# Dealing the two free PSUM banks of an attention by a fixed rule instead of in turns

## The reference, cut to what matters

```python
x = L0_attn_in_features                                # (8, 512, 256)
xn = _layernorm(x)
x = x + _L0_attn_ref(xn, ...) + _L0_ffn_ref(xn, ...)   # causal softmax attention; experts
xn = _layernorm(x)
x = x + _L1_attn_ref(xn, ...) + _L1_ffn_ref(xn, ...)   # gated recurrence; experts

def _L0_attn_ref(in_features, Wq, Wk, Wv, Wo):         # 16 heads of 16
    q, k, v = split_heads(xn @ Wq.T), ...
    scores = einsum('bhsd,bhtd->bhst', q, k) / 4       # causal mask
    out = einsum('bhst,bhtd->bhsd', softmax(scores), v)
    return out @ Wo.T
```

## Time and profile before

| | |
|---|---|
| time, median of 3 runs | 1647.87 us (1644.03 to 1649.47) |
| the profiled execution | 1642.28 us, span 1640.5 us |
| mean granted TensorE clock | 0.979 |
| TensorE busy | 1536.9 us (94%) |
| VectorE busy | 861.1 us (52%) |
| ScalarE busy | 733.3 us (45%) |
| GpSimd busy | 713.8 us (44%) |

### The profile page before, as it was taken

How to read it: one execution, slowest core, us unless ns; L and a number is a source line. 1 busy time by engine, 2 the same in 40 slices (tenths; PEclk the granted TensorE clock), 3 DMA queues, 4 the chain that set the end, 5 groups by cost and what they waited for, 6 DMA issues and landing times.

```text
span 1640.5 us, 32489 instructions
## 1 busy us (share of the span) xinstructions
PE 1536.9 (94%) x10874; PEld 1180.9 (72%) x10874; DVE 861.1 (52%) x2424; ACT 733.3 (45%) x1923; POOL 713.8 (44%) x815
## 2 busy tenths in 40 slices
PE   5888989999999999999988799998999999999997
PEld 3445445555547999998655467767999899999996
DVE  5777897787822444442577778874322122222220
ACT  4544545555551232333556466644333333334332
POOL 3132336676532555553810467753333333333332
PEclk9899999999999999999998999999999999999999
DMA  8534324435306444444622386467333333333331
GB/s 271 126 115 110 79 73 98 104 94 102 83 4 240 108 113 114 113 114 130 204 92 67 103 219 105 79 105 290 59 56 52 51 56 54 55 58 59 53 55 23
DMA packets 154640, 167.60 MB, mean 102 GB/s; under 512 B 84821, under 2 KB 132817, under 8 KB 151409
## 3 DMA queue, kind: packets, MB, share of 16 engines
q1 hardware_dynamic: 129936, 128.15, 31.5%
q0 software_dynamic: 24544, 37.38, 10.6%
HBM read 104.10 MB, written 44.45 MB: 91 GB/s over the span
## 4 chain that ended last, share of the span: by engine, by line
PE 78%; DVE 10%; DMA 4%; issue 3%; ACT 3%; SPq 1%; POOL 0%; another core or an unknown queue 0%; DVEq 0%; ACTq 0%; POOLq 0%
PE PS L1660 23%; PE PS L1678 22%; PE PS L1517 4%; PE PS L1453 3%; PE PS L1767 3%; DVE PS L1980 3%; PE PS L1502 3%; PE PS L1481 2%; PE PS L1634 2%; PE PS L1543 2%; PE PS L1588 2%; PE PS L1779 2%; PE PS L1463 1%; PE PS L1865 1%; DMA arena<-FD 1%
## 5 line engine op out<-in xcount | busy, mean ns | idle before, releaser
L1660 PEld LDWEIGHTS PS<-arena 128*128 128x128 f32 x3408 | 398.2, 192 | 16.3 <-DVE arena L2201 4.9
L1660 PE MATMUL PS<-arena 128*128 128x128 f32 x3408 | 405.3, 276 | 3.5 <-DVE arena L2201 3.5
L1678 PE MATMUL PS<-arena 128*128 x1704 | 392.3, 379 | 0.0
L1678 PEld LDWEIGHTS PS<-arena 128*128 128x128 f32 x1704 | 311.9, 190 | 40.1 <-issue 0.2
L1980 DVE CUSTOM_DVE_ANT_0 PS<-PS,arena 128x512 f32<-128x512 f32 (+3 forms) x512 | 235.2, 522 | 50.7 <-PE PS L1481 47.2
L995 POOL DMA_INDIRECT out<-arena x71 | 111.7, 1573 | 296.4 <-ACT arena L1272 274.0
L1262 ACT ACTIVATE arena<-PS,arena 128x128 f32<-128x128 f32 x568 | 161.8, 368 | 138.3 <-PE PS L1660 136.5
L2226 DVE COPY arena<-arena 128x8 f32 x71 | 12.2, 172 | 347.5 <-ACT arena L1262 326.3
L928 POOL TENSOR_SCALAR_AFFINE_SELECT arena<-arena 128x256 f32<-128x256 f32 x256 | 99.4, 411 | 204.0 <-ACT arena L1178 203.7
L981 POOL DMA_INDIRECT arena<-XN,arena x142 | 145.0, 1021 | 98.6 <-PE PS L1645 40.6
L1178 ACT ACTIVATE arena<-PS 128x512 f32<-128x512 f32 (+1 forms) x256 | 166.5, 705 | 42.1 <-PE PS L1502 34.4
(11 more groups left out here) (246 smaller groups left out, 2014.3 us busy)
## 6 DMA issues: line engine op xcount, KB each, us to landing
arena<-FD SPq DMA_DIRECT2D x32, 512.0 KB
arena<-in_w SPq DMA_DIRECT2D x16, 1024.0 KB
SPL<-arena SPq DMA_DIRECT2D x32, 384.0 KB, 2.6
arena<-SPL SPq DMA_DIRECT2D x64, 192.0 KB
XN<-arena SPq DMA_DIRECT2D x16, 512.0 KB, 3.0
arena<-SPL SPq DMA_DIRECT2D x64, 128.0 KB
arena<-SUM SPq DMA_DIRECT2D x16, 512.0 KB, 6.4
arena<-in_x SPq DMA_DIRECT2D x8, 512.0 KB, 6.6
```

Source lines behind the costliest of these rows:

```text
L1660: ins = pe.matmul(o, m.now[i % 2][:, c * F + 128 * f:c * F + 128 * f + 128], m.xt[i % 2][:, 128 * c:128 * c + 128], start=(c == 0), stop=( ...
L1678: ins = pe.matmul(to, m.hT[i % len(m.hT)][:, 128 * c:128 * c + 128], m.WD[:, bass.ds(e * (nf * 256) + c * 256, 256)], start=(c == 0), stop ...
```

## The change

A table gives each kind of small step a fixed bank; a kind with two entries takes the one of its last index (half or m). It holds from the step after the last `logitsT` on. Up to there, and for kinds that are not in the table, the turns are as before.

```diff
+OWN = {"scale": (7,), "project": (6, 7), "unscaleT": (7,), "maxrow": (6,), "output": (6, 7), "project_v": (6, 7)}
@@ def attention_banks(order):
-    uses, ring = Uses(), [4, 5, 6, 7]
+    uses, ring, own = Uses(), [4, 5, 6, 7], {}
     for step in order:
         if step[0] == "two_banks":
             ring = [7, 6]
             uses.at[step] = tuple(uses.count[b] for b in (4, 5))
+        elif step[0] in own:
+            uses.take(step, own[step[0]][step[-1] if len(own[step[0]]) > 1 else 0])
         elif step[0] in ("xt0", "xt1", "logits", "logitsT", "project", "project_v", "maxrow", "scale", "unscaleT", "output", "first_up", "first_down"):
             ring.append(ring.pop(0))
             uses.take(step, ring[-1])
+            if step == ("logitsT", NB - 1):
+                own = OWN
         elif step[0] == "values":
             uses.take(step, 6)
```

## The result

The changed kernel takes 1634.22 us (median of 11 runs, 1630.32 to 1638.53). The kernel before, run beside it, takes 1644.03 us (11 runs, 1636.31 to 1649.47). The ratio is 0.995, with a 95% interval from 0.9931 to 0.9968: 8.2 us gained, between 5.3 and 11.3. The forecast was 1642.2 us with a range from 1637 to 1648. Faster was right; the time lies under the range. The profiled execution took 1631.14 us (span 1629.4, clock 0.979), which is 11.1 us less than the one of before.

The account below looks back on a forecast made before the run. TensorE was taken to bound most of the first attention, VectorE weighing as much before it. Gains of 0.35 + 0.38 + 5.0 = 5.7 us off the 1647.87 us median gave 1642.2 us, range 1637 to 1648.

Parts of the forecast that it names:

- cost zero: Second project, bank 6 to 7: its new wait for the unscaleT copy delays nothing, with some 0.24 us of cover.
- values: Values in each round of 8 heads: the 0.36 us bank wait goes, and 0.33 us passes on through VectorE's gap.
- output, project_v: First output or project_v half of each round, bank 7 to 6: its 0.38 us wait goes in full.
- So the two gains add: Per round of 8 heads, the values' 0.33 us and the output's 0.38 us sum to 0.71 us.
- 7 rounds of 0.71 = 5.0 us: Gain claimed for the even stretch of the first attention, from 250 to 420 us.
- VectorE takes over: Rival, chance 0.13: VectorE swallows the values' gain everywhere, leaving 3.4 us gained, 1644.5 us.
- The early part: Before 250 us: the project at 174.46 gains 0.35 us, project_v at 185.8 gains 0.38, the rest taken as 0.
- Values at 180 us ... buys nothing: Before 250 us: VectorE has no gap from 178.78 to 188, so these values' 0.37 us gains nothing.
- Clock gains: Rival, chance 0.17: half-speed loss avoided at 174 us (1.7 us) or also later; 7.4 or 9.8 us gained, 1638 to 1640.5.
- Clock loses: Rival, chance 0.10: longer idling at the routing's end slows one more stretch by 2.4 us; 3.3 us gained, 1644.6.
- The new wait binds: Rival, chance 0.05: second project waits 1.07 us for the unscaleT copy at ten places; net 5.0 us slower, 1652.9.
- It does nothing: Rival, chance 0.05: the named releasers are wrong and data hold the same steps; 1647.9 us.

Follow-up runs that it names:

- e2: Kernel before with only the values' bank wait undone (both projects on bank 7); ratio to before 0.9993, slots 48–108 in 177.76 us.
- e1: Kernel before with only the second project's own bank wait undone; ratio to before 0.9984, slots 48–108 in 179.02 us.
- e3: Kernel before with only the output and project_v bank wait undone (halves on 6 and 7); ratio to before 0.9971, slots 48–108 in 176.87 us.
- e5: Kernel before with the values' and the output or project_v waits undone, the project's kept; 1639.37 us, slots 48–108 in 174.21 us.
- e4: Changed rule only from head slot 49 on, behind the routing, banks of before until then; ratio to before 0.9962, slots 48–108 in 173.79 us.
- e6: Kernel before with the project's and the output or project_v waits undone, the values' kept; 1632.61 us, slots 48–108 in 175.39 us.
- e8: The changed kernel run and profiled a second time, nothing altered; 1624.61 us, slots 48–108 in 173.80 us.
- e11: The changed kernel profiled a third time, nothing altered; 1629.05 us, slots 48–108 in 173.80 us.
- e12: Second profile, on another chip, of the kernel with the changed rule only from slot 49 on; 1628.02 us, slots 48–108 in 173.72 us.
- e9: Changed rule in head slots 25 to 48 only, banks of before from slot 49 on; ratio to before 0.9976, slots 48–108 in 180.52 us.

## Why the prediction was wrong

**The step that failed** is the project's: "TensorE itself arrives only at 308.32, straight from its scores", "cost zero", and with it the reading of idle time as the whole of a wait. 308.32 was no free arrival: the first project's subtract ends at 308.17 (307.48 + 0.69), and 0.15 us on, just what I had taken from the multiply to the output, the project starts. It was a bank wait that the overlap of the rows kept out of the list. I had stated in the text before that neighbouring rows overlap, and did not use it. The same error made the other two terms too small. For values there was a second one: VectorE's gap of 0.33 us, taken as the most that can pass on, did not bound the gain (0.42 in e2).

| term, per round | forecast | measured alone |
|---|---|---|
| second project | 0 | 0.24 (e1) |
| values | 0.33 | 0.42 (e2) |
| output, project_v | 0.38 | 0.55 (e3) |
| all three | 0.71 | 0.96 (changed, 6.73 / 7) |

"So the two gains add" was nearly right (e5: 6.50 of 6.79). "7 rounds of 0.71 = 5.0 us" should have been 6.7. The 16 heads that took 48.75 us (262.98 to 311.73) take 46.89 in the changed kernel (257.81 to 304.70): 1.86 us less, where 1.4 were named as the sign.

**VectorE takes over** was a rival, and came true in a small place: in the changed kernel VectorE took back most of the project's gain, in the half of the round with the output. Rows of e5 (project's wait kept), timeline of the same kind of round:

```profile
306.94 0.69 DVE L1971 TENSOR_TENSOR arena<-PS,arena 128x512 f32<-128x512 f32 x1 [0.50 <-ACT arena L1156]
307.29 2.36 PE L1522 MATMUL PS<-arena 128*32 128x512 f32 x32
...
308.96 1.09 POOL L937 TENSOR_TENSOR arena<-arena 128x512 bf16<-128x512 f32 x1
...
309.94 0.18 DVE L1992 CAST arena<-arena 128x32 bf16<-128x32 f32 x1
...
312.10 0.86 PE L1486 MATMUL PS<-arena 96*128 96x512 bf16 x4
...
312.79 1.95 PE L1548 MATMUL PS<-arena 128*128 128x256 f32 x8
...
318.59 2.36 PE L1522 MATMUL PS<-arena 128*32 128x512 f32 x32
```

Groups by line, that cast from 250 to 400 us (busy us, mean ns, idle before), kernel before:

```profile
L1987 DVE CAST arena<-arena 128x32 bf16<-128x32 f32 x6 | 1.1, 181 | 0.2
```

The changed kernel:

```profile
L1992 DVE CAST arena<-arena 128x32 bf16<-128x32 f32 x6 | 2.0, 333 | 0.2
```

Kernel e1:

```profile
L1992 DVE CAST arena<-arena 128x32 bf16<-128x32 f32 x6 | 2.0, 339 | 0.2
```

The cast takes 0.33 us in place of 0.18 where the project's wait is gone (the same in e4, e6, e8, e11 and e12) and 0.18 where it is kept (before three times, e2, e3, e5, e9). In both rounds it starts 2.65 us after values (307.35 - 304.70, 309.94 - 307.29), but GpSimd's subtraction, which follows its row before without idle time, starts 1.85 us after values in the changed one and 1.67 in e5 (306.55 - 304.70, 308.96 - 307.29). So the cast starts 0.28 us before GpSimd's low part ends (306.55 + 1.08 = 307.63), and itself ends at 307.68. In e5 it starts only 0.11 us before GpSimd's end (310.05), and ends at 310.12.

VectorE's next passes come 0.15 us later against TensorE, and the scores before the output, which wait for them, show it: from scores to output 0.69 us in e5 (312.10 to 312.79), 0.85 in the changed kernel (309.51 to 310.36). From values to the next values that is 11.30 us in e5 (307.29 to 318.59) and 11.46 in the changed kernel (304.70 to 316.16): 0.16 of the 0.22 us are gone again. The longer cast costs that only where VectorE has no idle time left behind it. In e6 it is as long, but values start later there and VectorE's next pass still waits for its scores; the half takes 11.30 us. Timeline of e6, VectorE:

```profile
307.87 0.34 DVE L1992 CAST arena<-arena 128x32 bf16<-128x32 f32 x1
...
309.05 0.70 DVE L1985 CUSTOM_DVE_ANT_0 PS<-PS,arena 128x512 f32<-128x512 f32 x1 [0.17 <-PE PS L1486]
```

The Trainium skill, SBUF — State Buffer, section "Who interferes with whom", says that VectorE and GpSimd share one pair of ports as an exclusive lock, that a cast can take this pair where its operands allow one of the two-port modes, and that the engine that comes later is then blocked until the other's instruction is over. The traces agree. Over all 14 profiles this cast is in 224 places. In 85 no GpSimd row runs beside it, and it takes 0.16 to 0.18 us. In 63 a GpSimd subtraction has 0.28 to 0.45 us left when the cast starts, and it takes 0.33 to 0.49 and ends 0.04 to 0.05 us behind that subtraction, whatever was left. In the rest GpSimd has at most 0.12 us left, or starts later, and it takes 0.18. So where the subtraction has that long to go, the cast ends with it: that the rows show. No row says which mode the cast runs in, and no run took GpSimd's low part away, so the lock as the reason stays argued.

**The early part.** Forecast: 0.35 us from the project at slot 27, 0.38 from project_v, nothing else. Slots 24–28 gain 0.68 us without the clock (e12's 15.31 to 14.63), again more than the listed wait (from scores to project 1.01 us in e12, 0.59 in e9: 0.42). "Values at 180 us ... buys nothing" was a second term at nothing: e2, where values are free and the project's wait is kept, takes 14.87 us in 24–28 against 15.31 in e12, and does not give these 0.44 us back in 28–44 (51.89 against 51.84). Slots 28–44 gain 0.54 us in the changed kernel (forecast 0.38).

**The clock**, of which I took nothing, went both ways, so two rivals came true in part. *Clock gains*, at its first place: the project at slot 27 took 3.65 us in before and 1.96 in e9, and that is 1.70 us of slots 24–28 (17.01 to 15.31) wherever slots 20–24 were long. The rival had 1.7 for it; where they were short there was no fall to save. *Clock loses*, at the second: slots 44–48 took 18.83 to 18.87 us in before and e4, and 19.13 to 20.20 in the four profiles with the rule ahead of them. TensorE comes earlier to the routing's end, and VectorE's work there does not: TensorE's longest wait for it, in these slots ahead of a scores row, grew from 1.86 to 3.32 us. Timeline of before, then of the changed kernel:

```profile
236.28 0.38 PE L1481 MATMUL PS<-arena 96*128 96x512 bf16 x1 [1.86 <-DVE arena L1980]
```

```profile
231.85 1.50 PE L1486 MATMUL PS<-arena 96*128 96x512 bf16 x4 [3.32 <-DVE arena L1985]
```

In the changed kernel TensorE does 0.15 us of work from 230 to 232 us, and the clock is at 0.50 from 232 on (first fence); a mean of 0.84 over 230 to 232 puts the fall at about 231.4, 5.8 us behind the values of slot 44 (225.52 + 5.8). In before it comes at 239.4, 8.0 us behind those values (231.40). So the half speed begins some 2 us sooner, and it takes more of these slots. Windows from values of slot 44 to values of slot 48, before and then changed:

```profile
231.40:250.24 18.84, 14.57 (x89) 8.87 (x89) 14.55 (x54) 6.51 (x12) 7.90 (x12) 0.82 0.23 67
225.52:245.72 20.20, 15.25 (x90) 9.13 (x89) 15.97 (x55) 6.65 (x13) 7.60 (x12) 0.75 0.23 66
```

It does not take more of them each time: the changed kernel again has 0.75 in e8 (20.19 us) but 0.82 in e11 (19.13 us, where 20.2 was expected). So the loss is 0.3 to 1.4 us, where the rival had 2.4. Nor does it come with every part of the rule: e1, e2 and e6 took 18.44, 18.12 and 18.69 us here, less than before, and e3 and e5 19.03 and 19.39.

The Trainium skill, TensorE: Matmul & The Clock Gate, section "A second HAM failure mode: psum-queue depth-cycling", tells of a bf16 kernel; carried over to this one, it would have the bank waits bring the half speed. At slot 27 one run (e9) is on its side, after a long 20–24; over the even stretch, with all its 14 waits, the clock was 1.00.

**The sum, made again**: 6.7 to 6.8 (even stretch), 0.7 (or 2.4, where slots 20–24 are long), 0.5, less 0.3 to 1.4: 6.5 to 9.4 us, beside the 8.2 (5.3 to 11.3) of the ratio and a forecast of 5.7.

**The base.** The forecast was set against a median of three runs, 1647.87. Over 11 runs beside the changed kernel before takes 1644.03, and beside the experiments 1637.78 to 1639.63. So 3.8 of the 8.0 us of the miss are the base (1647.87 - 1644.03), and 4.1 the sum (9.8 between the medians, less 5.7). The profiled execution, 1642.28, was nearer than the median that I chose. On the base of 1644.03 the forecast would have been 1638.3, still 4.1 us over the measured time.

*The new wait binds*: no project waits for the unscaleT copy, whose row ends at 301.55 in the changed round, against a start at 301.80. *It does nothing*: no.

## What to carry to other kernels

A wait for a bank is the distance from the start of the step ahead to the start of the blocked one, less the same distance where nothing blocks; the idle time in the list is smaller, and a wait can hide altogether (0.14 us here with nothing listed). Give a step whose reader is late a bank that the next step does not need, and expect the gains of neighbouring waits to add only until another engine sets the pace: here each pair that was run added nearly in full, and the third wait brought little. Set a forecast against as many executions as there are, the profiled one among them.

## What the runs showed that was not expected

- The same kernel (e4, e12) spends 18.10 or 16.47 us in slots 20–24, and slots 24–28, with the same wait of 0.35 us in slot 27, then take 17.00 or 15.31 us.
- After a long 20–24 the clock fell at a single wait of 0.35 us (six profiles) and did not fall without it (one, e9), while 14 waits of that length in the even stretch left it at 1.00.
- A cast of 128x32 takes 0.18 or 0.33 us, by whether it starts 0.11 or 0.28 us before a GpSimd subtraction ends, and the difference costs TensorE nothing or 0.16 us a round, by whether VectorE has idle time behind it.
